# Convolutions and recurrence one batch further ahead of the attention, with a third buffer for h, earlier x loads and a rewritten end

## The reference, cut to what matters

```python
z, f, o = tanh(conv(W_z)), sigmoid(conv(W_f)), sigmoid(conv(W_o))
c = f * c + (1 - f) * z;  h = o * c          # along the tokens
h = h + attention(layernorm(h))
out = h + experts(layernorm(h))              # gate weight zero once an expert is full
```

## Time and profile before

| | us |
|---|---|
| three executions, median (lowest to highest) | 437.19 (436.45 to 437.37) |
| the profiled execution, its own time | 434.99 |
| span of the profiled execution, first to last instruction | 433.2 |
| granted TensorE clock, mean | 0.994 |
| busy: PE / DVE / POOL / ACT | 410.9 / 387.0 / 372.9 / 323.6 |
| DMA moved | 56.08 MB, mean 129 GB/s |

### The profile page before, as it was taken

How to read it: one execution, slowest core, us unless ns; L and a number is a source line. 1 busy time by engine, 2 the same in 40 slices (tenths; PEclk the granted TensorE clock), 3 DMA queues, 4 the chain that set the end, 5 groups by cost and what they waited for, 6 DMA issues and landing times.

```text
span 433.2 us, 12681 instructions
## 1 busy us (share of the span) xinstructions
PE 410.9 (95%) x4554; PEld 280.3 (65%) x4554; DVE 387.0 (89%) x873; ACT 323.6 (75%) x728; POOL 372.9 (86%) x389
## 2 busy tenths in 40 slices
PE   8789899999999999999999999999999999998884
PEld 5444364776757676776767677676757676766763
DVE  4487999899999999999999999999999999999563
ACT  3756677879687877968687887868788796858773
POOL 7596999999989989898998989898998999997611
PEclk9999899999999999999999999999999999999999
DMA  8330757452726365363726446182734537164500
GB/s 287 130 102 3 196 148 198 103 173 61 200 81 156 107 148 153 81 171 99 196 68 145 145 115 188 50 196 81 170 108 120 164 96 201 41 192 125 143 12 24
DMA packets 78703, 56.08 MB, mean 129 GB/s; under 512 B 28305, under 2 KB 71345, under 8 KB 78513
## 3 DMA queue, kind: packets, MB, share of 16 engines
q1 hardware_dynamic: 78640, 55.28, 47.2%
HBM read 35.56 MB, written 19.70 MB: 128 GB/s over the span
## 4 chain that ended last, share of the span: by engine, by line
PE 78%; DVE 11%; issue 4%; ACT 2%; DMA 2%; POOL 2%; SPq 0%; DVEq 0%; POOLq 0%; ACTq 0%
PE bank L450 20%; PE bank L539 9%; PE bank L516 8%; PE bank L400 6%; PE bank L426 6%; PE bank L401 5%; PE bank L478 5%; PE bank L466 4%; DVE prod L1228 4%; PE bank L458 3%; PE bank L508 2%; PE bank L493 2%; PE bank L418 2%; PE bank L434 2%; PE bank L411 1%
## 5 line engine op out<-in xcount | busy, mean ns | idle before, releaser
L1698 POOL TENSOR_TENSOR prod<-q,k 128x1496 f32<-128x1496 f32 x48 | 144.5, 3028 | 21.8 <-ACT k L852 16.1
L1228 DVE SCALAR_TENSOR_TENSOR prod<-bank,par,k 128x1496 f32<-128x1496 f32 x80 | 140.8, 1766 | 0.0
L450 PE MATMUL bank<-prod,ew 128*32 128x374 f32 x1024 | 87.3, 479 | 1.7 <-ACT gate L859 1.0
L1683 POOL TENSOR_TENSOR fprod<-q,k 128x374 f32<-128x374 f32 (+6 forms) x112 | 80.3, 753 | 0.0
L450 PEld LDWEIGHTS bank<-prod,ew 128*32 128x32 f32 x1024 | 31.3, 109 | 47.1 <-issue 41.1
L953 ACT ACTIVATE hid<-bank,par 128x374 f32<-128x374 f32 x64 | 36.3, 575 | 23.5 <-PE bank L516 21.7
L786 ACT ACT_TABLE_LOAD x40 | 51.3, 1283 | 1.4 <-PEq L1918 0.7
L516 PE MATMUL bank<-x,par 128*128 128x374 f32 x128 | 48.3, 483 | 1.9 <-ACT x L906 1.9
L539 PE MATMUL bank<-par,hid 128*128 128x128 f32 x384 | 47.9, 276 | 0.0
L539 PEld LDWEIGHTS bank<-par,hid 128*128 128x128 f32 x384 | 45.9, 192 | 2.6
L400 PE MATMUL bank<-xT,par 128*128 128x374 f32 x96 | 41.2, 511 | 3.7 <-DMA xT<-x_dram 3.1
(11 more groups left out here) (119 smaller groups left out, 876.8 us busy)
## 6 DMA issues: line engine op xcount, KB each, us to landing
band<-band_scratch SPq DMA_DIRECT2D x16, 768.0 KB, 5.2
band_scratch<-attn SPq DMA_DIRECT2D x64, 180.4 KB, 3.0
vnear<-v_scratch SPq DMA_DIRECT2D x48, 192.0 KB, 2.9
v<-v_scratch SPq DMA_DIRECT2D x32, 192.0 KB, 4.1
v_scratch<-vtok SPq DMA_DIRECT2D x16, 192.0 KB, 3.0
xT<-x_dram SPq DMA_DIRECT2D x16, 187.5 KB, 3.4
vfar<-v_scratch SPq DMA_DIRECT2D x16, 128.0 KB, 3.3
out_dram<-osb SPq DMA_DIRECT2D x16, 128.0 KB
```

The source lines that it names most:

```text
L450: done = mm(home(f"s{c}")[32 * g:32 * g + 32, lo:N], ew[:, c * CW + j, :], src[:, j, lo:N], start=first or only, stop=last or only)
L1228: v.scalar_tensor_tensor(bass.AP(prod[c][:, :, :].tensor, part * N, [[CW * N, 128], [PARTS * N, w], [1, N]]), home("q")[:, 0:N].unsqueeze( ...
L1683: last = g.tensor_tensor(fprod[:, i, o:N], q[q_.s][:, o:N], k[q_.s][:, KPAD:KPAD + N - o], ALU.mult)
L1698: g.tensor_tensor(bass.AP(prod[c][:, :, :].tensor, part * N, [[CW * N, 128], [PARTS * N, w], [1, N]]), q[q_.s][:, :].unsqueeze(1).broadcas ...
```

## The change

The convolutions and the recurrence of a batch run one turn earlier relative to all the rest of it. In the turns every lag but 0 and 1 grows by one (`a2` becomes `a3`, `a3` becomes `a4` and so on), and the turns run to one number higher; the work of a turn and its order on each engine stay the same. So the written-out part at the start has one more batch of convolutions and recurrence in it, and the turns with the highest numbers have one less. `h` gets a third buffer, since one more batch of it is alive, and its end pad is cleared in a third place. x of batch 1 is loaded ahead of the parameters, and x of batch 2 ahead of the zeroing of the scratch areas. At the start on ScalarE and VectorE some calls change places, and the first turn of both is written out (on VectorE with one reciprocal moved behind a block of products). At the end two calls move: `turn_o(seq[14])` ahead of two feed-forward calls, and `carry(seq[15])` ahead of the last `far_sum(seq[14], 5)`.

```diff
+HBUF = 3
-        h = [sb(f"h{s}", [128, NP]) for s in range(2)]
+        h = [sb(f"h{s}", [128, NP]) for s in range(HBUF)]
...
             load_x(Seq(0, 0, 0))
+            load_x(Seq(1, 1, 0))
             sp.dma_start(par[:, cut:PCOLS], params[:, cut:PCOLS]).then_inc(par_in, 16)
...
-            load_x(Seq(1, 1, 0))
+            load_x(Seq(2, 0, 1))
 
             sp.wait_ge(pads_zero, 1)
...
-            load_x(seq[2])
             load_x(seq[3])
-            write_values(seq[0])
             load_x(seq[4])
+            write_values(seq[0])
+            load_x(seq[5])
...
-            pipeline(sp, turn, range(5, 17))
+            pipeline(sp, turn, range(6, 18))
```

TensorE, start, then the turns (each lag above 1 one higher, with the same calls in the same order), then the end:

```diff
             convolve(seq[2], 0, ("z", seq[1]), head=True)
             convolve(seq[2], 1, ("f", seq[1]))
             turn_x(seq[0])
-            project(seq[0], "k", ("o", seq[1]), head=True)
+            convolve(seq[2], 2, ("o", seq[1]))
+            convolve(seq[3], 0, ("z", seq[2]), head=True)
+            convolve(seq[3], 1, ("f", seq[2]))
+            project(seq[0], "k", ("o", seq[2]), head=True)
             project(seq[0], "q")
-            convolve(seq[3], 0, ("z", seq[2]), head=True)
-            convolve(seq[2], 2, ("k", seq[0]))
-            value_project(seq[0], ("f", seq[2]))
-            convolve(seq[3], 1, ("v", seq[0]))
+            convolve(seq[4], 0, ("z", seq[3]), head=True)
+            convolve(seq[3], 2, ("k", seq[0]))
+            value_project(seq[0], ("f", seq[3]))
+            convolve(seq[4], 1, ("v", seq[0]))
...
-                if a2:
-                    turn_h(a2, ("ht", a3))
+                if a3:
+                    turn_h(a3, ("ht", a4))
...
-            pipeline(pe, turn, range(6, 18))
+            pipeline(pe, turn, range(7, 19))
...
             up(seq[13], 3, ("x2b", seq[13]), head=True)
+            turn_o(seq[14], ("pv", seq[14]))
             logits(seq[13], ("tb2", seq[14]))
             up(seq[13], 0, ("tb1", seq[14]))
-            turn_o(seq[14], ("pv", seq[14]))
```

ScalarE, start:

```diff
             norm1_ln(seq[0])
             norm1_exp(seq[0])
+            norm1_rows(seq[0])
             tanh_o(seq[1])
-            norm1_rows(seq[0])
-            norm1_back(seq[0])
             tanh_z(seq[2])
             tanh_f(seq[2])
+            half_forget(seq[2])
+            tanh_o(seq[2])
+            norm1_back(seq[0])
+            tanh_z(seq[3])
+            tanh_f(seq[3])
             copy_k(seq[0])
             copy_q(seq[0])
-            half_forget(seq[2])
-            tanh_o(seq[2])
+            half_forget(seq[3])
+            tanh_o(seq[3])
             value_rows(seq[0])
             keep_rows(seq[0])
-            tanh_z(seq[3])
...
+            tanh_z(seq[4])
...
             norm1_ln(seq[1])
-            score_copy(seq[0], 1)
             norm1_exp(seq[1])
             norm1_rows(seq[1])
+            score_copy(seq[0], 1)
```

VectorE, the buffer of h and the start:

```diff
-                after(dve, h_turned, q_.b - 1)
-                v.scalar_tensor_tensor(h[q_.s][:, 0:N], ...
+                after(dve, h_turned, q_.b - HBUF + 1)
+                v.scalar_tensor_tensor(h[q_.b % HBUF][:, 0:N], ...
...
             stats1(seq[0])
+            shift_rows(seq[0])
             recur_in(seq[1])
             recur(seq[1])
-            shift_rows(seq[0])
             recur_out(seq[1])
             recur_in(seq[2])
             recur(seq[2])
+            recur_out(seq[2])
+            recur_in(seq[3])
+            recur(seq[3])
             products(seq[0], 0, 1, head=True)
             products(seq[0], 1, 0)
             stats1(seq[1])
             products(seq[0], 0, 2)
-            recur_out(seq[2])
-            recur_in(seq[3])
+            recur_out(seq[3])
+            recur_in(seq[4])
```

GpSimd, the end:

```diff
             far_sum(seq[14], 4)
+            carry(seq[15])
             far_sum(seq[14], 5)
-            carry(seq[15])
             far_sum(seq[15], 1)
```

More of the change, by code:

```diff
@@ L561, in turn @@
[L561 to L584, removed]
@@ L1062, in _ @@
             score_copy(seq[1], 0)
-            pipeline(act, turn, range(5, 17))
+            score_copy(seq[1], 2)
+            norm1_back(seq[2])
+            open_gate(seq[1])
+            band_copy(seq[0], 0)
+            band_copy(seq[0], 2)
+            copy_k(seq[2])
+            copy_q(seq[2])
+            band_copy(seq[0], 1)
+            softmax_dense(seq[1])
+            softmax_far(seq[1])
+            tanh_o(seq[5])
+            value_rows(seq[2])
+            keep_rows(seq[2])
+            tanh_z(seq[6])
+            tanh_gate(seq[2])
+            tanh_f(seq[6])
+            norm2_ln(seq[0])
+            norm1_ln(seq[3])
+            norm1_exp(seq[3])
+            norm2_exp(seq[0])
+            half_forget(seq[6])
+            softmax_exp(seq[1])
+            score_copy(seq[2], 1)
+            norm2_rows(seq[0])
+            norm1_rows(seq[3])
+            score_copy(seq[2], 0)
+            pipeline(act, turn, range(7, 18))
             score_copy(seq[13], 2)
@@ L1487, in _ @@
             stats1(seq[2])
-            recur_in(seq[4])
+            recur_in(seq[5])
             products(seq[1], 0, 0)
@@ L1510, in _ @@
             stats1(seq[3])
-            recur_out(seq[4])
-            recur_in(seq[5])
+            recur_out(seq[5])
+            recur_in(seq[6])
             products(seq[2], 0, 0)
@@ L1517, in _ @@
             softmax_sum(seq[1])
-            recur(seq[5])
+            recur(seq[6])
             score_add(seq[2], 1)
             score_add(seq[2], 0)
-            pipeline(dve, turn, range(6, 17))
+            score_add(seq[2], 2)
+            score_max(seq[2])
+            score_subtract(seq[2])
+            products(seq[3], 0, 1, head=True)
+            softmax_rcp(seq[1])
+            attention_sum(seq[1])
+            attention_norm(seq[1])
+            near_values(seq[2])
+            recur_out(seq[6])
+            attention_gate(seq[1])
+            route_max(seq[0])
+            products(seq[3], 1, 0)
+            route_picks(seq[0])
+            route_mask(seq[0])
+            residual(seq[1])
+            products(seq[3], 0, 2)
+            keep(seq[0])
+            stats2(seq[1])
+            stats1(seq[4])
+            recur_in(seq[7])
+            take_room(seq[0])
+            products(seq[3], 0, 0)
+            shift2_rows(seq[1])
+            shift_rows(seq[4])
+            products(seq[3], 0, 3)
+            gate_sum(seq[0])
+            add_b2(seq[0])
+            gate_weight(seq[0])
+            softmax_sum(seq[2])
+            recur(seq[7])
+            finish(seq[0])
+            score_add(seq[3], 1)
+            score_add(seq[3], 0)
+            pipeline(dve, turn, range(8, 18))
             score_add(seq[13], 2)
@@ L1635, in _ @@
                 g.memset(xn[s][:, N:NP], 0.0)
+            for s in range(HBUF):
                 g.memset(h[s][:, N:NP], 0.0)
@@ L1814, in _ @@
             far_products(seq[3], 0)
-            pipeline(pool, turn, range(6, 17))
+            pipeline(pool, turn, range(7, 18))
             kept_mask(seq[11])
```

400 lines of the change are left out of this document (212 added, 188 removed).

## The result

The changed kernel takes 439.88 us (median of 22 runs, 436.52 to 442.5), the kernel before, timed beside it on the same chip, 436.55 us (22 runs). The ratio is **1.0074**, 95% interval 1.0055 to 1.0093: slower by 0.7%. Seven of the 22 runs, with a mean granted clock of 0.993, took 436.52 to 437.22 us, the others, at 0.980 to 0.990, 438.6 to 442.5. Its profiled execution took 440.35 us with a span of 438.6 us, 5.36 us more than that of before (434.99 us).

The account below looks back on a forecast made before the run. TensorE bounds the full turns, GpSimd and VectorE the turns without convolutions. Start +3.2 and end -1.67 make +1.53 us; on a median of 437.19 that gives 438.7 us, 0.35% slower, range 436.0 to 440.3.

Parts of the forecast that it names:

- TensorE as the limit of the full turns, GpSimd behind it: Turns: TensorE gapless for 24.90 us in a full turn; without convolutions the limit passes to GpSimd and VectorE.
- The end's gain of 2.34 us, GpSimd's two waits: Last turns: GpSimd gains only its waits of 0.94 and 1.40 us; after the early carry 1.67 us remain.
- The first rival: Last turns: TensorE stays the limit to the end, which gains 4.06 us, giving 436.3 us in all; chance 0.16.
- the swallowed start: Between 36.5 and 45.3 us: waits of GpSimd and TensorE absorb the 3.2 us delay, giving 435.5 us; chance 0.12.
- The z convolution of batch 2: Start: it waits for recur_in behind shift_rows and setup, starting at 16.9 us; 0.4 us is lost.
- The term "3.2 us" for the start: Start, second half: k and q of batch 0 arrive 3.2 us later, all carried to the turns; bounds 2.8 and 5.1.
- The queues: Start, SyncE loads: all moves about 1.7 us, x of batch 3 lands near 18.1, before use at 21.1; no cost.
- The early carry: End, GpSimd: carry of batch 15 ahead of batch 14's last sum takes 0.99 us, cutting the gain to 1.67 us.
- turn_o "within 0.3 either way": End, TensorE: turn_o of batch 14 ahead of two products counts for nothing, within 0.3 us either way.
- the +0.9 to +1.5 us that the forecast gave: Whole kernel: +1.53 us is the forecast sum; +0.9 us is the rival that the moved carry is free, chance 0.12.

Follow-up runs that it names:

- the filler: Changed kernel with eight matmuls on constants, result overwritten, put into TensorE's wait ahead of the z convolution of batch 2: 438.22 us, 1.0038 of the kernel before.
- kernel A: Changed kernel with shift_rows and both end edits undone, and tanh_o of batch 1 back ahead of norm1_rows of batch 0 on ScalarE: 434.55 us, 0.9967.
- shift_rows undone: Changed kernel with shift_rows of batch 0 and its setup back behind the recurrence of batch 1 on VectorE: 437.01 us, 1.0015.

## Why the prediction was right, and where not

Forecast: 438.7 us and slower; measured 439.88, in the range. The direction and most of the mechanism were right; the nearness of the number was partly luck. The forecast put the change at +1.5 us, and it is +3.3 in the medians and +5.36 between the two profiled executions. The forecast median came close because it stood on a median of before that was itself 0.6 us higher than in the later runs.

- **TensorE as the limit of the full turns, GpSimd behind it.** Right. The turn without z and f came one earlier and lasts 22.73 us, where 22.5 was forecast. The forecast had GpSimd gapless in all three last turns; in this first one it still waits 1.40 us for k, until 309.31. Behind that it has no wait up to the last sums.
- **The end's gain of 2.34 us, GpSimd's two waits.** Right, a little small. The two waits of 0.94 and 1.40 us that rows 9 shows at 318.44 and 329.11 are gone. The lag of `attention_sum` behind the kernel before falls from 5.08 us, where it stands from 107 to 306 us, to 2.93, 2.29 and 2.28 in the last turns: 2.80. The other 0.46 is not waiting of GpSimd but 0.56 us less busy time in the three windows; what shortened it no run shows.
- **The first rival, TensorE to the end for 4.06 us,** doesn't hold, and neither does the swallowed start: GpSimd's second block came 5.39 us later, and all but 0.3 of that went on to the turns.
- **The z convolution of batch 2.** The mechanism was the one forecast, a wait for `recur_in` behind `shift_rows` and the setup, at 17.39 (16.9 forecast). The step that failed is its price, 0.4 us. I set the new wait against the old wait for x and called the difference the cost. But the new wait also left TensorE idle for 3.73 us in one piece, and the clock went down to 1.2 GHz on the products behind it: 1.45 us each instead of 0.79. The term "3.2 us" for the start measured 5.39: from that convolution to k it took 8.37 us, where 3.78 + 2.82 = 6.60 was forecast. Of the 1.77 us too many, 1.64 is what the filler took out.
- **What undoing the line is worth** was also missed: 2.9 us of start in the profiles, 1.64 of it the clock. My sum compared with the kernel before, in which x was late; against the kernel with its x on time, the order alone cost as much as the turns gained.
- **ScalarE's order**, `norm1_rows` ahead of `tanh_o` of batch 1, was not priced. It costs 0.54 us once VectorE's order is right.
- **The queues.** Right: x of batch 3 came in time, TensorE never waited for it.
- **The early carry** was put at 0.67 us (0.99 of work, 0.32 of it covered). The comparison of traces gives 0.98 (lag at `attention_sum` 3.26 us after 2.28), kernel A with and without it 0.87.
- **turn_o "within 0.3 either way".** Right: 0.11 us in kernel A. Beside the early carry it waits 0.99 us for onorm, and even so the two cost no more than the carry alone (0.84 to 0.90 us) while the clock stays at 1.00.
- **The clock at the end** had no term. In the profiled execution it fell in that wait of 0.99 us and cost 34.21 - 32.12 = 2.09 us, the largest single term of the end. The order of the calls doesn't decide this by itself. With shift_rows undone, the end is the same code with the same two waits, and the clock stays at 1.00:

```profile
397.09 0.87 PE L518 MATMUL bank<-x,par 128*128 128x374 f32 x2 [1.27 <-ACT x L911]
398.95 0.52 PE L488 MATMUL bank<-par,onorm 128*128 128x128 f32 x3 [0.99 <-DVE onorm L1328]
...
399.92 2.10 PE L518 MATMUL bank<-x,par 128*128 128x374 f32 x6
```

The run with the wait filled shows the same (1.26 and 1.00 us, 2.10). Three profiles have this end, and in one of them the clock fell; why in that one is open.

The sum of the traces closes: arrival -0.64; start +2.59 for the moved convolutions, +0.54 for ScalarE's order, +2.91 for VectorE's with what the clock adds to it; the rest -2.95 for kernel A against before (the turns, and about 0.3 of the clock near 46 us), +0.84 for the early carry, +2.09 for the clock at the end. Together +5.38, measured +5.36. Seven runs of the kernel after at a mean clock of 0.993 took 436.5 to 437.2 us, near the +0.9 to +1.5 us that the forecast gave. They are not free of the lower clock: the run with both end edits undone, whose end kept 1.00 in its trace, reads 0.990 to 0.995, kernel A 0.996 to 1.000. They would fit without the fall at the end, but no trace of such a run exists, and what decides it is open.

The Trainium skill ("Perfetto Trace Analysis", section "Optimization Strategy") says that a kernel whose most contended engine changes over time may get faster when these stretches are interleaved. The runs agree only once the orders at the start and the end were mended: 0.9972 and 0.9967, against 1.0074.

## What to carry to other kernels

When prefetch work moves into a start that is a chain of latencies, look on each engine for what a waiting instruction now stands in front of: one line on VectorE cost as much as the deeper pipeline won. Price a new long wait of TensorE twice, for its length and for the products behind it at half clock. And before taking work off the way to the first block, find out whether the first or the second block sets the pace.

## What the runs showed of the hardware

A TensorE wait of 3.73 us was followed, after 1.2 us of work, by about 3.4 us at a granted clock of 0.50. In two other kernels, with waits of 3.87 and 4.20 us, the clock fell before the wait was over and stayed at 0.50 for some 6.4 us. Eight useless matmuls in the wait kept the clock at 1.00, and the kernel was faster with them, 1.0038 against 1.0074, with intervals that just touch.

The surprise was that equal short waits are followed by either clock. Waits of 1.26 and 0.99 us within three microseconds (399.18 and 401.03) came with a clock of 0.50 from about 400.9 to 407.6 us in the kernel after; the same two waits in the runs with shift_rows undone and with the wait filled, with 1.00. A wait of 2.25 us for near values, between 45 and 56 us, was followed by 0.50 in these two runs (2.59 us before), and by 1.00 in the other traces of changed kernels. So a short gap cost 2 us in one trace of this code and nothing in two others.

Small VectorE operations of one shape scatter as well: `hbias` on 128x12 elements lasted 0.85 us in kernel A, 1.01 after, 2.37 before and 3.82 with shift_rows undone, and the four operations of the setup took 1.04 to 2.20 us together. No run shows why.

The start's scatter was larger than I expected: the z convolution of batch 1 begins between 9.25 and 11.44 us in thirteen profiled executions, and all of it is in the time. For edits worth less than 1 us the distances inside a trace said more than medians of 12 runs.
